# Routing signs turned on VectorE, the conv's current tap on ScalarE, and the denominator's terms moved ahead of the squares' sums

## What is computed

```python
x = silu(x_prev * conv_w[:, 0] + x * conv_w[:, 1])      # x_prev: the token before, along the 8 batches
q, k, v, g = silu(x @ Wq), x @ Wk, x @ Wv, x @ Wg       # 16 heads: 32 wide (q, k), 64 wide (v, g)
q, k = rotary(q), rotary(k)
route = argmax(v @ router_w)                            # one of 2 per token and head
qk = (q @ k.T) * [route equal] * coefficient * tril     # coefficient: score / running count
o = layernorm(qk @ v)
out = (silu(g) * o) @ Wout
```

## Time and profile before

| | |
|---|---|
| median of 3 runs | 1704.71 us (1703.75 to 1705.87) |
| profiled execution | 1703.55 us, span 1701.8 us |
| granted TensorE clock, mean | 0.977 of 2.4 GHz |
| busy: TensorE, VectorE, ScalarE, GpSimd | 1559.1, 1482.6, 721.4, 599.8 us |
| share of the span | 92%, 87%, 42%, 35% |
| DMA | 70.73 MB, mean 42 GB/s |

### The profile page before, as it was taken

How to read it: one execution, slowest core, us unless ns; L and a number is a source line. 1 busy time by engine, 2 the same in 40 slices (tenths; PEclk the granted TensorE clock), 3 DMA queues, 4 the chain that set the end, 5 groups by cost and what they waited for, 6 DMA issues and landing times.

```text
span 1701.8 us, 37091 instructions
## 1 busy us (share of the span) xinstructions
PE 1559.1 (92%) x15607; PEld 795.4 (47%) x15607; DVE 1482.6 (87%) x1984; ACT 721.4 (42%) x901; POOL 599.8 (35%) x715
## 2 busy tenths in 40 slices
PE   0425999999999999999999999999999999999997
PEld 0112445555554555555555555555455555555454
DVE  7888888888998888889988888899888888899842
ACT  4825434444344344443444443443443444434421
POOL 1421344333343443323434443324444433334320
PEclk9957899999999999999999999999999999999999
DMA  9500011101101111111011111001111111010000
GB/s 270 204 13 0 26 39 39 39 27 28 36 26 38 39 38 39 31 27 33 27 37 39 38 39 39 26 26 35 29 38 39 39 39 28 28 36 26 26 14 25
DMA packets 23549, 70.73 MB, mean 42 GB/s; under 512 B 2264, under 2 KB 2520, under 8 KB 23384
## 3 DMA queue, kind: packets, MB, share of 16 engines
q1 hardware_dynamic: 23384, 68.37, 13.8%
HBM read 51.59 MB, written 16.78 MB: 40 GB/s over the span
## 4 chain that ended last, share of the span: by engine, by line
DVE 72%; issue 11%; ACT 11%; PE 5%; DVEq 0%; DMA 0%; POOL 0%; SPq 0%; ACTq 0%
DVE seg L866 10%; DVE small L847 5%; DVE seg L857 4%; DVE big L314 4%; DVE fb L859 3%; ACT ek L625 3%; DVE x_ring L1035 2%; DVE fa L859 2%; DVE big L1075 2%; DVE fa L1029 2%; DVE fb L1025 2%; DVE fb L876 2%; DVE seg L1061 2%; ACT L625 2%; DVE fb L1019 2%
## 5 line engine op out<-in xcount | busy, mean ns | idle before, releaser
L394 PE MATMUL ps_g<-big,h_hi 128*128 128x512 f16 x1536 | 586.6, 382 | 12.4 <-issue 6.1
L398 PE MATMUL ps_g<-big,h_lo 128*128 128x512 f16 x1536 | 586.2, 382 | 3.1 <-DVE big L1075 3.1
L395 PE MATMUL ps_g<-big,h_hi 128*128 128x512 f16 x1536 | 586.4, 382 | 0.0
L394 PEld LDWEIGHTS ps_g<-big,h_hi 128*128 128x128 f16 x1536 | 156.4, 102 | 185.3 <-issue 19.1
L398 PEld LDWEIGHTS ps_g<-big,h_lo 128*128 128x128 f16 x1536 | 151.0, 98 | 187.3 <-issue 8.1
L1209 POOL TENSOR_TENSOR small<-small 128x1 f32<-128x1 f32 x64 | 14.3, 223 | 612.5 <-DVE small L851 612.4
L395 PEld LDWEIGHTS ps_g<-big,h_hi 128*128 128x128 f16 x1536 | 150.9, 98 | 165.3 <-issue 4.6
L394 PE MATMUL ps_g<-big 128*128 128x512 f16 x512 | 195.0, 381 | 15.6 <-DVE big L941 15.6
L395 PE MATMUL ps_g<-big 128*128 128x512 f16 x512 | 194.7, 380 | 0.0
L398 PE MATMUL ps_g<-big 128*128 128x512 f16 x512 | 194.6, 380 | 0.0
L866 DVE TENSOR_TENSOR_SCAN seg<-decay,seg 128x1088 f32<-128x1088 f32 x64 | 177.2, 2768 | 2.2
(11 more groups left out here) (169 smaller groups left out, 2699.5 us busy)
## 6 DMA issues: line engine op xcount, KB each, us to landing
x_ring<-in_x SPq DMA_DIRECT2D x32, 512.0 KB
vx<-in_ctx SPq DMA_DIRECT2D x32, 512.0 KB
out<-x_ring SPq DMA_DIRECT2D x31, 512.0 KB
big<-in_wv SPq DMA_DIRECT2D x2, 2048.0 KB, 21.2
big<-in_wg SPq DMA_DIRECT2D x2, 2048.0 KB, 20.8
big<-in_wout SPq DMA_DIRECT2D x2, 2048.0 KB, 20.0
big<-in_wq SPq DMA_DIRECT2D x1, 2048.0 KB, 14.3
big<-in_wk SPq DMA_DIRECT2D x1, 2048.0 KB, 19.4
```

The lines of the kernel that those rows point to most:

```text
L394: nc.tensor.matmul(dst[:, :], hi, hi_of(u)[:, kc * HALF:(kc + 1) * HALF], start=(kc == 0), stop=False)
L395: nc.tensor.matmul(dst[:, :], hi, lo_of(u)[:, kc * HALF:(kc + 1) * HALF], start=False, stop=False)
L398: last = nc.tensor.matmul(dst[:, :], lo, hi_of(u)[:, kc * HALF:(kc + 1) * HALF], start=False, stop=(kc == KC - 1))
```

## The change

Three things:
1. The signs are turned on VectorE. GpSimd's `route` is now sign times `seen` (`seen` is the row sum of the former `reach` by position in a block of 32). VectorE transposes `route` in blocks of 32x32 (`turn_heads`, bf16, 128x512) into `sgn_t`, which lies in the scratch `tmp`, and `same` compares that. The `same_route` matmul, `reach` and `fold` go; `gate_max_turn` waits for `s_us` in place of `s_same`.
2. The conv. ScalarE makes the current tap's product (`conv_now`: eight copies of 128 columns from PSUM, scaled by `cw1`), and VectorE adds the past tap in one fused instruction per chunk of 128 (`conv_past`: eight instructions of 112 elements). Silu and split go by halves.
3. VectorE's `denominator_terms(n)` stand first in its step, ahead of `final(i - 2, 1)` and the sums of squares.

```diff
-        reach = work[:, ...].bitcast(BF16)
-        fold = work[:, 3 * C + HALF // 2 + P // 2:3 * C + HALF // 2 + P // 2 + BLK]
+        seen = work[:, 3 * C + HALF // 2 + P // 2:3 * C + HALF // 2 + P // 2 + BLK]
+        sgn_t = tmp[:, 0:HALF // 2].bitcast(BF16)
...
@@ tensor: step, gate_max_turn
-                    same_route(i)
-                after(pe, s_same, p + 1)
+                after(pe, s_us, p)
-            def same_route(i):
-                after(pe, s_route, i + 1)
-                after(pe, s_us, i)
-                nc.tensor.matmul(ps_s[1][:, :], reach, route, start=True, stop=True).then_inc(s_rt, 1)
@@ scalar: step, and the opening with n = 0
                     normed_x(n, (slot + 1) % 4)
-                    silu_h(n)
-                    split_h(n, 0)
-                    split_h(n, 1)
+                    conv_now(n)
+                    for g in range(2):
+                        silu_h(n, g)
+                        split_h(n, g)
+            def conv_now(n):
+                act.wait_ge(s_x2, n + 1)
+                for g in range(2):
+                    act.wait_ge(s_xnp, 2 * n + g + 1)
+                    for c in range(4):
+                        k = 4 * g + c
+                        last = A(fa[:, k * P:(k + 1) * P], ps_t[g][:, c * P:(c + 1) * P], ACT.Copy, scale=cw1[:, k:k + 1])
+                    last.then_inc(s_z, 1)
+            def silu_h(n, g):
+                part = slice(g * HALF, (g + 1) * HALF)
+                act.wait_ge(s_pre, 2 * n + g + 1)
+                A(fa[:, part], fa[:, part], ACT.Silu).then_inc(s_h, 1)
@@ vector: step
                 n, p = i + 1, i - 1
+                if nxt:
+                    denominator_terms(n)
...
                 if nxt:
-                    denominator_terms(n)
                     denominator_scan(n)
...
                     turn_heads(s_rk, i, rot_k, k_sb, s_kt)
+                    turn_heads(s_route, i, route, sgn_t, s_rt)
                     same(i)
...
-                    conv_products(n, 0)
-                    conv_products(n, 1)
-                    conv_sum(n)
+                    conv_past(n)
@@ vector: denominator_terms
-                after(dve, s_pre, n)
+                after(dve, s_hhi, 2 * n)
+            def conv_past(n):
+                for g in range(2):
+                    dve.wait_ge(s_z, 2 * n + g + 1)
+                    for c in range(4):
+                        k = 4 * g + c
+                        now = fa[:, k * P:(k + 1) * P].rearrange("p (r b) -> p r b", b=NB)[:, :, 1:NB]
+                        past = ps_t[g][:, c * P:(c + 1) * P].rearrange("p (r b) -> p r b", b=NB)[:, :, 0:NB - 1]
+                        last = V.scalar_tensor_tensor(now, past, cw0[:, k:k + 1], now, ALU.mult, ALU.add)
+                    last.then_inc(s_pre, 1)
@@ vector: same
-                V.tensor_tensor(by_head(same_m, BLK), by_head(ps_s[1][:, :], BLK), per_head(sgn, 0, H, BLK),
+                V.tensor_tensor(by_head(same_m, BLK), by_head(sgn_t, BLK), per_head(sgn, 0, H, BLK),
@@ vector: tokens_by_time, and gpsimd: route
-                V.tensor_copy(reach, ps_t[0][:, 0:P]).then_inc(s_tc, 1)
+                V.tensor_reduce(seen, ps_t[0][:, 0:P].rearrange("p (n l) -> p l n", l=BLK), AX_X, ALU.add).then_inc(s_tc, 1)
-                V.tensor_reduce(fold, ident[:, :].rearrange("p (n l) -> p l n", l=BLK), AX_X, ALU.add)\
-                 .then_inc(s_tc, 1)
-                                    fold.rearrange("p (o l) -> p o l", o=1).to_broadcast([P, H, BLK]), ALU.mult)\
+                                    seen.rearrange("p (o l) -> p o l", o=1).to_broadcast([P, H, BLK]), ALU.mult)\
```

More of the change, by code:

```diff
@@ L122, in flamingo_layer @@
         route = work[:, 3 * C:3 * C + HALF // 2].bitcast(BF16)
-        reach = work[:, 3 * C + HALF // 2:3 * C + HALF // 2 + P // 2].bitcast(BF16)
-        fold = work[:, 3 * C + HALF // 2 + P // 2:3 * C + HALF // 2 + P // 2 + BLK]
+        seen = work[:, 3 * C + HALF // 2 + P // 2:3 * C + HALF // 2 + P // 2 + BLK]
         turn = work[:, 3 * C + HALF:4 * C]
@@ L221, in flamingo_layer @@
             ("bn2", "aggr2", "rstd2", "nbias2", "xn_done"))
-        s_z, s_z2, s_pre, s_h, s_hhi, s_hlo = (sem(n) for n in
-            ("conv_now", "conv_past", "conv_done", "h_done", "h_hi_done", "h_lo_done"))
+        s_z, s_pre, s_h, s_hhi, s_hlo = (sem(n) for n in
+            ("conv_now", "conv_done", "h_done", "h_hi_done", "h_lo_done"))
         s_q, s_k, s_vc = sem("q_copied"), sem("k_copied"), sem("v_copied")
@@ L234, in flamingo_layer @@
         s_p, s_route, s_rt, s_same = (sem(n) for n in
-            ("probs_done", "route_signs", "route_matmul", "same_route"))
+            ("probs_done", "route_signs", "route_signs_turned", "same_route"))
         s_gmt = sem("gate_max_by_batch")
@@ L578, in _ @@
             nc.tensor.transpose(ps_t[0][:, 0:P], causal_m[:, :], ident[:, :]).then_inc(s_tp, 1)
-            pe.wait_ge(s_tc, 8)
+            pe.wait_ge(s_tc, 7)
             xn_transposes(0, False)
@@ L709, in normed_x @@
                     A(vx[:, part], x_ring[:, slot, part], ACT.Identity, scale=rs2, bias=nb2).then_inc(s_xn, 1)
-            def silu_h(n):
-                act.wait_ge(s_pre, n + 1)
-                A(fa[:, :], fa[:, :], ACT.Silu).then_inc(s_h, 1)
+            def conv_now(n):
[10 more added lines that the diff above has]
+                A(fa[:, part], fa[:, part], ACT.Silu).then_inc(s_h, 1)
             def split_h(n, g):
-                act.wait_ge(s_h, n + 1)
+                act.wait_ge(s_h, 2 * n + g + 1)
                 after(act, s_gp, 2 * n)
@@ L745, in _ @@
             split_unit(1)
-            silu_h(0)
-            split_h(0, 0)
-            split_h(0, 1)
+            conv_now(0)
+            for g in range(2):
+                silu_h(0, g)
+                split_h(0, g)
             exp_k(1, 1)
@@ L1037, in residual @@
                 norm_stats(n, xs, st2, mv2, s_bn2, s_ag2)
-            def conv_sum(n):
-                dve.wait_ge(s_z, 2 * (n + 1))
-                dve.wait_ge(s_z2, 2 * (n + 1))
-                now = fa[:, :].rearrange("p (r b) -> p r b", b=NB)[:, :, 1:NB]
-                past = seg[:, 0:C].rearrange("p (r b) -> p r b", b=NB)[:, :, 0:NB - 1]
-                V.tensor_tensor(now, now, past, ALU.add).then_inc(s_pre, 1)
+            def conv_past(n):
+                for g in range(2):
+                    dve.wait_ge(s_z, 2 * n + g + 1)
[5 more added lines that the diff above has]
+                    last.then_inc(s_pre, 1)
             def h_low(n):
@@ L1052, in h_low @@
                                            ALU.mult, ALU.subtract).then_inc(s_hlo, 1)
-            def conv_products(n, g):
-                dve.wait_ge(s_x2, n + 1)
-                dve.wait_ge(s_num, n + 1)
-                dve.wait_ge(s_xnp, 2 * n + g + 1)
-                V.tensor_tensor(fa[:, g * HALF:(g + 1) * HALF].rearrange("p (c n) -> p c n", n=P),
-                                ps_t[g][:, :].rearrange("p (c n) -> p c n", n=P),
-                                per_chunk(cw1, 4 * g, 4 * g + 4, P), ALU.mult).then_inc(s_z, 1)
-                V.tensor_tensor(seg[:, g * HALF:(g + 1) * HALF].rearrange("p (c n) -> p c n", n=P),
-                                ps_t[g][:, :].rearrange("p (c n) -> p c n", n=P),
-                                per_chunk(cw0, 4 * g, 4 * g + 4, P), ALU.mult).then_inc(s_z2, 1)
             def same(i):
@@ L1166, in _ @@
             lo_unit(0)
-            conv_products(0, 0)
-            conv_products(0, 1)
-            conv_sum(0)
+            conv_past(0)
             spread(3, 2)
@@ L1292, in _ @@
             router_products(1)
-            pool.wait_ge(s_tc, 8)
+            pool.wait_ge(s_tc, 7)
             pipeline(pool, step)
```

## The result

The changed kernel takes 1749.9 us (median of 4 runs, 1749.7 to 1752.8) against 1704.2 for the kernel before on the same chip: ratio 1.027, 95% interval 1.026 to 1.029. It is slower by 45.6 us, outside the range that was forecast. These are the page's lines for the engines and for TensorE's out projection; the last two columns of a group are the idle time just before it and what ended most of that. The second fence has the same group of the kernel before.

A forecast was written before the change was run, and what follows sets the result against it. Bound: TensorE's 47.87 us of work and a VectorE chain, nearly equal in a 48.30 us period. Per step +0.04, so +1.2 over 29 periods, +3.0 opening, -2.3 steps 0 and 1, -0.2 last step: +1.7, 1706.4 us; range 1688 to 1721.

The forecast's parts named there:

- Part 1: Terms ahead of the squares' sums, and the conv: both shorten VectorE's way to `signs`, which start 0.80 us earlier per step.
- part 2: VectorE's row behind the earlier `signs`: waits for GpSimd total 2.48 us instead of 2.26, 0.22 more; bounds 1.5 to 3.3.
- L964 slips in ahead, its 0.87 is gone.: Small VectorE instruction behind `signs`: runs before GpSimd's rotation of k, so its 0.87 us wait disappears.
- Part 3: Signs turned on VectorE: one bf16 transpose ahead of L941 adds 0.62 us per step (0.35 to 0.70); comparison unchanged.
- rival A: Faster: the transpose is cheap (0.35 us, about 1698) or the waits also fall well (about 1687); chance 0.31.
- The sum: Per step -0.80 + 0.22 + 0.62 = +0.04 us, period 48.34; with opening, steps 0 and 1 and last step, +1.7 in all.
- the opening: Start of the kernel: VectorE waits for ScalarE's copies, so `h_low` starts later; +3.0 us, between 1.5 and 3.7.
- steps 0 and 1: TensorE's early waits for `h_lo` (2.85) and L941 (1.78): the earlier conv saves 2.3 us net of the transpose.
- three signs of being wrong: Period 47.66 with no wait for L941 (A), L859 near 2.5 (B), or `signs` without an idle stretch ahead (C).
- B: Slower: GpSimd's sum gets in before L859 at the turn of v; 0.4 us more per step, about 1718; chance 0.2.
- C: Slower: terms lose to GpSimd's product, q's rotation meets the gate's product, the 0.80 is lost; about 1723; chance 0.09.

The follow-up runs named there:

- b1: The kernel before with the conv part alone (current tap on ScalarE, past tap fused on VectorE, silu and split by halves): 1705.3 us, ratio 1.001.
- h1: g2 with GpSimd's factors multiplying the squared coefficients by 1/DV ahead of the wait for the squares' sum: 1706.6 us, ratio 1.001.
- g2: The changed kernel with the second half of `final` moved from ahead of the squares' sum to between it and the scan: 1707.7 us, ratio 1.002.
- g1: The changed kernel with two unused statistics instructions on VectorE between the squares' sum and the denominator's scan: 1715.6 us, ratio 1.007.
- b2: The kernel before with the turned signs alone: 1721.3 us, ratio 1.010.
- e1: The changed kernel with the denominator's terms behind the squares' sum again: 1720.1 us, ratio 1.009.
- e2: The changed kernel with the signs spread by TensorE's matmul again, no transpose of them on VectorE: 1722.9 us, ratio 1.011.
- f1: e1 with the turn of the signs and the comparison `same` moved behind `gt_lo`, ahead of the mask: 1700.9 us, ratio 0.998.
- f2: The changed kernel with the turn of the signs and the comparison moved behind the low part of the gate: 1726.9 us, ratio 1.014.
- g3: g1 with the turn of the signs and the comparison moved behind the low part of the gate, ahead of the mask: 1725.5 us, ratio 1.013.
- e3: The changed kernel with the conv undone (four products and the sum on VectorE, silu in one piece): 1791.5 us, ratio 1.051.
- b3: The kernel before with the denominator's terms ahead of the sum of squares alone: 1788.0 us, ratio 1.049.

## Why the prediction was wrong

**Part 1 held.** `signs` start at 24.74, as forecast to the hundredth. VectorE is ready at 838.55 + 0.69 = 839.24, 22.2 into the period (forecast 22.3 to 23.4, so just ahead of it). The exp ends at 11.04 instead of 10.6, because the copies and the fused instructions took their upper bounds:

```profile
820.33 2.17 ACT L711 ACTIVATE fa<-ps_t,small 128x128 f32<-128x128 f32 x8 [1.00 <-PE ps_t L386]
...
821.50 2.09 DVE L1052 SCALAR_TENSOR_TENSOR fa<-ps_t,small,fa 128x112 f32<-128x112 f32 x8 [0.22 <-ACT fa L711]
```

That is 2.09 where I took 1.5, and it cost nothing (b1). The terms did win the race against GpSimd's product of the values, 828.11 against 828.16.

**The step that failed is in part 2: "L964 slips in ahead, its 0.87 is gone."** It rests on a sentence of part 1, that the rotation of q "now comes before GpSimd's long product". That is true (L314 takes 0.68), and it is the trouble: the product that no longer meets the rotation meets `signs`. The prediction gives the gate's product no place of its own and doesn't ask what stood between the sum and the scan. At its old distance of 5.45 behind the sum it would have ended at 833.39 + 5.45 + 2.76 = 841.60 (an estimate from these rows), just ahead of `signs` at 841.78. The terms that part 1 moves had been GpSimd's window. L964 (now L969) waits 1.38 instead of 0. The other waits came out at 0.54, 0, 0.95 and 0.67 for the forecast 0.85, 0, 0.96 and 0.65; the last one fell on the carry copy, not on the state's sum (L876). In all 3.54 against 2.48 (the four terms of the forecast add up to 2.46), outside my bounds of 1.5 to 3.3. h1 confirms the step from the other side: with the gate's product out of the way the waits are 2.48 and the period is 48.26, where 48.34 had been forecast.

**Part 3 held.** The two transposes, the new bf16 one among them, take 1.30 us in one stretch, so 0.60 for the second, and the comparison 0.69 as before:

```profile
808.95 1.30 DVE L1072 STREAM_TRANSPOSE big<-big 128x512 f32<-128x512 f32 x2
810.28 0.69 DVE L1066 TENSOR_TENSOR big<-big,small 128x512 f32<-128x512 bf16 x1
```

The Trainium skill (VectorE: DVE Perf Modes, Mode 2x_1P) lets dense 16-bit operands go two per cycle; this transpose, 16-bit on both sides, does not show it: all 32 of them take 0.67, the f32 ones 0.70. The cheap transpose of rival A did not come.

**The sum.** With 3.54 for 2.48 the step is +0.04 + 1.06 = +1.10; measured +1.02 in the periods without a clock fall. Of the opening the +3.0 was right (TensorE's transposes of step 1 at 174.03 against 170.81, +3.2), but steps 0 and 1 gave back 0.4 instead of 2.3: the wait for `h_lo` fell from 2.85 to 0.26, and this came back as a longer wait for `gt_lo`, 4.50 for 1.78:

```profile
219.54 0.58 PE L394 MATMUL ps_g<-big 128*128 128x512 f16 x1 [4.50 <-DVE big L948]
```

**The term that was missing** is the clock, 13.7 us. I priced TensorE's idle time as idle time alone. **Of the rivals** none came true, and none of the three signs of being wrong appeared. B's place (L859 against GpSimd's sum) was won as forecast, at 1.23. C has the meeting with the gate's product, but put it at the rotation and asked for late terms. A mechanism that starts from GpSimd's side of the sum was not among them, and the slow end of the range was set by waits that the trace of before already showed.

## What to carry to other kernels

When an instruction is moved, ask what the other engine did while it ran: work that leaves a shared port free can be the window in which someone else's short, urgent instructions get through. If a reduction releases small work on GpSimd, put something with one SBUF input between it and the next long instruction with two. How much of the small work slips through does not tell what it is worth: g2 let two factors through and gained 1.03 per step, g1 let four through and gained 0.8, because its power was stretched. And where a forecast lets TensorE stand still longer in each step than before, price its clock too: here, with 1.65 us for 0.43, that raised the loss by almost a half.

## What the runs showed that was not expected

- GpSimd instructions of 16 elements (0.22 us) are shut out for the full rest of a scan (2.26 us), like long ones.
- A wait taken from one instruction can come back at the next: in h1 0.35 less at L971 became 0.33 more at the carry copy.
- TensorE's clock by the idle stretch in front of the out projection: with 0.4 to 1.35 us of it (before, b1, b2, e1, e2, f1, f2, g1, g2, g3, h1) the steady periods show no fall, nor do the few single stretches of 1.5 to 1.7 us in b2, e1, f2 and g3; with 1.65 us 7 of the 28 steady periods of the changed kernel do (the two stretches of 2.0 us that it has are among them), with 2.06 us (e3) nearly all, with 2.3 us ahead of another matmul (b3) about every second. In the changed kernel each fall lasted some 3.4 us and cost 1.7. Why one period with 1.65 has it and the next has not stayed open.
